# Half-array row scores, value products woven between the scores of a slot, and another buffer in the convolution

## The chip, the cores and the metric

The kernel runs on one core of one Trainium2 chip. The metric is the device time of one execution in microseconds (us), lower is better. Engines: PE (TensorE, matrix products), DVE (VectorE), ACT (ScalarE), POOL (GpSimd), and SP, which issues DMAs.

## What is computed

Two layers over an input of 4 batches x 1024 positions x 256 channels. Layer 0: a long convolution between gates, then a feed-forward network with weights reduced to signs. Layer 1: causal attention with 16 query heads over 4 key heads of 64 channels, then a mixture of experts. Every part stands behind a layer norm and is added to the input through a gate. Cut to the parts that the change touches:

```python
# layer 0, convolution
up = einsum('bld,de->ble', u, in_w) + in_b                  # e = 768: x0, x1, v of 256 channels each
uc = depthwise causal convolution of up with 3 taps, + short_b
vx = v * x1
y = irfft(rfft(vx) * rfft(k)) + vx * filt_bias              # long convolution
out = (y * x0) @ out_w + out_b
# layer 1, attention
scores = einsum('bkgqd,bkpd->bkgqp', qg, k) * scale
probs = softmax(where(causal, scores, -1e30))
out = einsum('bkgqp,bkpd->bkgqd', probs, v)
```

## The kernel before

Batches run one after the other (`for bi in range(B)`), and each engine has its own instruction stream written out by hand; semaphores tie them together. PE's stream in a batch is: convolution, feed-forward, projections, attention, output, experts.

**Attention.** For a head u of 1024 queries the scores are computed twice. `score_rows(u, i)` (L577) computes queries i x 128 to (i + 1) x 128 against the keys up to them, as rows; DVE's `row_maxima` (L1239) takes the row maximum from them. `score_cols(u, c, j)` (L600) computes the transposed scores of keys j x 128 against a half c of 512 queries; the exponential needs the row maximum, which is subtracted by an extra row of the product. Values are split into a high and a low part of fp32r to keep precision: qhh holds the high part of q twice (partitions 0 to 63 and 64 to 127), khl the high part of k over its low part, so that one 128-row product gives q_high x (k_high + k_low); k2 and q2 have 65 rows, k_high over ones and q_low over the negated maxima. Where the block lies on the diagonal, a third product adds the causal mask (L617). The blocks of a head (`BLOCKS`) are 12 slots n = 0 to 11: four key tiles for queries 0 to 511 (512, 384, 256 and 128 columns wide) and eight for queries 512 to 1023 (512 wide five times, 384, 256, 128). Slots 0 to 3 and 8 to 11 carry a mask; slots 3 and 11 are the narrow ones of 128 columns.

`values(u, c, j)` (L620) multiplies the exponentials (high and low part, psplit) with the values (vhi, vlo; 65 columns of weights), in three products (L631, L632, L634) into one of the two banks 0 and 1. It runs four slots behind the scores (`LAG`). `rows_at(u, n)` (L61) says which row scores of later heads a slot takes: tiles 4 to 7 of head u + 1 in slots 0 to 3, tiles 0 to 3 of head u + 2 in slots 8 to 11, one each; in head 0 slots 0 to 3 take two tiles of head 1 each. A row product of over 512 keys is two matmuls into two neighbouring banks. A slot on PE is: scores (high, low, mask), perhaps a projection (L450), row scores, perhaps the transposition of the maxima (L598), three value products of the slot four before. ACT writes each exponential twice (L942, L943); the low part is the difference, on DVE or POOL.

**Convolution.** The six channel tiles of `up` run in the order `E_ORDER`: v of tile 0, x1 of tile 0, v of tile 1, x1 of tile 1, x0 of both. PE projects one (`up_rows`, 12 matmuls), ACT writes it scaled by the last tap (L976), POOL corrects its first two columns (L1534), DVE adds the two other taps in two passes (L1327, L1330). `vx` is v times x1: tile 0 on POOL (L1537), tile 1 on DVE (L1335). There is one buffer x1 for both tiles, so ACT waits at n = 3 for the first product. `gated_rows` on PE (L636) transposes vx for the spectra (L661).

## Time and profile before

| | |
|---|---|
| median of 3 runs | 1879.77 us (1877.68 to 1879.78) |
| profiled execution | 1884.41 us, of which the span from first to last instruction is 1882.6 us |
| mean granted clock of PE in it | 0.968 of full |
| busy: PE, DVE, ACT, POOL | 1764.5, 1431.3, 1000.6, 695.8 us |
| share of PE in the chain that ended last | 65% |

The chain that ended last is followed back from the last instruction to what released each step. PE's recorded duration of a product holds its way through the array too; products overlap in it, so that the distance from start to start is what one costs. "PEld" is the load of weights, which runs beside the product before.

### The profile page before, as it was taken

What the parts mean: (1) busy time and instruction counts of PE and PEld (TensorE: products, weight loads), DVE (VectorE), ACT (ScalarE), POOL (GpSimd) and SP (SyncE); (2) the same over time, 40 slices, a digit from 0 to 9 for tenths busy, and PEclk for the clock granted to TensorE, in tenths of its full rate; (3) what the DMA queues carried; (4) which work ended last, traced back from release to release, by engine and by line L of the source; (5) the groups of instructions that cost most, each with busy time, mean ns of one, the idle gap of its engine ahead of it and who ended that gap; (6) DMA issues with size and microseconds to landing.
All of it is one profiled execution on the core that took longest, in us unless ns stands there. A gap on an engine that the chain in (4) does not pass through costs nothing.

```text
span 1882.6 us, 27319 instructions
## 1 busy us (share of the span) xinstructions
PE 1764.5 (94%) x9228; PEld 1427.0 (76%) x9228; DVE 1431.3 (76%) x2646; ACT 1000.6 (53%) x2162; POOL 695.8 (37%) x725
## 2 busy tenths in 40 slices
PE   8999799999998889999999979999999897999998
PEld 5778577778877767777877867777787785777787
DVE  6788778875678878887468877887656887788754
ACT  2314477676333356777441436777824244777752
POOL 1041444543231344444224144554323324445322
PEclk8999899999999989999999979999999998999999
DMA  7500534432610064343160044444143006354311
GB/s 282 195 7 1 134 108 130 130 69 52 230 56 1 20 168 117 91 133 76 53 250 1 1 118 124 114 102 109 45 169 129 0 1 173 86 135 124 75 30 51
DMA packets 89103, 183.09 MB, mean 97 GB/s; under 512 B 28991, under 2 KB 42111, under 8 KB 85894
## 3 DMA queue, kind: packets, MB, share of 16 engines
q1 hardware_dynamic: 84512, 169.55, 31.1%
q10 hardware_dynamic: 4454, 11.81, 2.0%
q8 instruction: 75, 1.23, 0.3%
q14 instruction: 62, 0.51, 0.1%
HBM read 124.41 MB, written 46.94 MB: 91 GB/s over the span
## 4 chain that ended last, share of the span: by engine, by line
PE 65%; DVE 13%; issue 6%; ACT 5%; DMA 3%; POOL 3%; DVEq 2%; ACTq 2%; SPq 0%; POOLq 0%
PE ps L450 10%; PE ps L591 7%; PE ps L611 7%; PE ps L613 6%; PE ps L634 6%; PE ps L631 6%; PE ps L632 6%; PE ps L804 4%; PE ps L725 3%; PE ps L456 3%; PE ps L680 3%; DVE oT L1260 2%; DVE psplit L1249 2%; PE ps L617 2%; PE ps L548 1%
## 5 line engine op out<-in xcount | busy, mean ns | idle before, releaser
L1239 DVE CUSTOM_DVE_ANT_0 ps<-ps,mrow 128x128 f32<-128x128 f32 (+7 forms) x512 | 385.4, 765 | 104.6 <-PE ps L591 103.0
L1509 POOL TENSOR_TENSOR psplit<-pT,psplit 128x384 fp32r<-128x384 f32 (+3 forms) x320 | 301.9, 957 | 422.6 <-ACT psplit L943 417.5
L943 ACT ACTIVATE psplit<-ps 128x512 fp32r<-128x512 f32 (+3 forms) x768 | 373.0, 486 | 0.0
L942 ACT ACTIVATE pT<-ps 128x512 f32<-128x512 f32 (+3 forms) x512 | 256.2, 500 | 174.0 <-PE ps L617 94.0
L591 PE MATMUL ps<-khl,qhh 128*128 128x512 f32 (+3 forms) x768 | 252.1, 393 | 39.1 <-DMA qhh<-psplit 25.0
L611 PE MATMUL ps<-qhh,khl 128*128 128x512 f32 (+3 forms) x768 | 270.7, 352 | 6.5 <-DMA q<-nmr 6.1
L613 PE MATMUL ps<-q,k 65*128 65x512 f32 (+3 forms) x768 | 268.0, 349 | 0.0
L631 PE MATMUL ps<-psplit,vhi 128*65 128x512 f32 (+3 forms) x768 | 264.2, 344 | 0.0
L634 PE MATMUL ps<-psplit,vhi 128*65 128x512 f32 (+3 forms) x768 | 259.5, 338 | 0.0
L632 PE MATMUL ps<-psplit,vlo 128*65 128x512 f32 (+3 forms) x768 | 259.0, 337 | 0.0
L611 PEld LDWEIGHTS ps<-qhh,khl 128*128 128x128 f32 x768 | 145.3, 189 | 58.3 <-issue 8.7
L591 PEld LDWEIGHTS ps<-khl,qhh 128*128 128x128 f32 x768 | 132.4, 202 | 57.0 <-issue 36.2
L1249 DVE TENSOR_TENSOR psplit<-pT,psplit 128x512 fp32r<-128x512 f32 x192 | 131.1, 707 | 42.3 <-ACT psplit L943 41.4
L942 ACT ACTIVATE mix<-ps 128x512 f32<-128x512 f32 (+2 forms) x256 | 118.1, 461 | 78.2 <-PE ps L613 46.4
L613 PEld LDWEIGHTS ps<-q,k 65*128 65x128 f32 x768 | 145.7, 190 | 17.0
L634 PEld LDWEIGHTS ps<-psplit,vhi 128*65 128x65 f32 x768 | 104.2, 136 | 43.1 <-issue 0.4
L1249 DVE TENSOR_TENSOR psplit<-mix,psplit 128x512 fp32r<-128x512 f32 x128 | 101.5, 793 | 42.1 <-ACT psplit L943 42.1
L632 PEld LDWEIGHTS ps<-psplit,vlo 128*65 128x65 f32 x768 | 104.7, 136 | 34.9
L898 ACT ACTIVATE work<-ps,modb 128x512 f32<-128x512 f32 x48 | 37.3, 778 | 173.5 <-PE ps L548 173.5
L450 PE MATMUL ps<-hT,wqkv 128*128 128x512 f32 x480 | 123.4, 411 | 6.2 <-DVE hT L1150 6.2
L631 PEld LDWEIGHTS ps<-psplit,vhi 128*65 128x65 f32 x768 | 105.5, 137 | 28.5 <-issue 0.3
L1260 DVE TENSOR_TENSOR oT<-work,mix 64x1024 f32<-64x1024 f32 x64 | 94.3, 1474 | 40.5 <-DMA mix<-inverse_scratch 39.6
(211 smaller groups left out, 3302.3 us busy)
## 6 DMA issues: line engine op xcount, KB each, us to landing
qhh<-q_scratch SPq DMA_DIRECT2D x112, 256.0 KB, 5.1
q_scratch<-hrow SPq DMA_DIRECT2D x24, 1024.0 KB, 6.9
mix<-inverse_scratch SPq DMA_DIRECT2D x64, 256.0 KB, 3.5
q<-q_scratch SPq DMA_DIRECT2D x56, 256.0 KB, 4.4
Kf<-kf_scratch SPq DMA_DIRECT2D x3, 3072.0 KB, 17.6
khl<-k_scratch SPq DMA_DIRECT2D x24, 256.0 KB, 7.5
sgn<-sgn_scratch SPq DMA_DIRECT2D x6, 1024.0 KB, 10.7
in_w<-in_w_scratch SPq DMA_DIRECT2D x3, 1536.0 KB, 6.7
```

The lines of the kernel that those rows point to most:

```text
L450: i = mm(o, lhs(a, q), rhs(c, q), start=n == 0, stop=n == len(pairs) - 1)
L591: q = mm(ps[:, b + c // HALF, 0:e - c], qhh[:, r, i * P:(i + 1) * P], khl[:, g % 2, c:e], start=True, stop=True)
L611: mm(ps[:, b, 0:hi - lo], khl[:, g % 2, j * P:(j + 1) * P], qhh[:, r, lo:hi], start=True, stop=False)
L613: i = mm(ps[:, b, 0:hi - lo], k2[:, g % 2, j * P:(j + 1) * P], q2[:, u % 2, lo:hi], start=False, stop=not diagonal)
L631: mm(o, vhi[:, g, j, :], high, start=j == 0, stop=False)
L632: mm(o, vlo[:, g, j, :], high, start=False, stop=False)
L634: mm(o, vhi[:, g, j, :], low, start=False, stop=j == 4 * c + 3).then_inc(s["pv_done"], 1)
L942: A(full(n)[:, 0:hi - lo], ps[:, b, 0:hi - lo], ACT.Exp, scale=SCALE)
L943: A(psplit[:, n % PRING, 0, 0:hi - lo], ps[:, b, 0:hi - lo], ACT.Exp, scale=SCALE)\
L1239: V.tensor_tensor_reduce(out=v, in0=v, in1=mrow[:, L - n:L], scale=1.0, scalar=-3e38, op0=ALU.add, op1=ALU.max, accum_out=mx[:, u % 2, i:i ...
L1249: V.tensor_tensor(psplit[:, n % PRING, 1, 0:m], full(n)[:, 0:m], psplit[:, n % PRING, 0, 0:m].bitcast(F32), ALU.subtract)\
L1509: G.tensor_tensor(psplit[:, n % PRING, 1, 0:m], full(n)[:, 0:m], psplit[:, n % PRING, 0, 0:m].bitcast(F32), ALU.subtract)\
```

## The change

Four things, all in one version. Row scores of heads 1 to 15 use 64 rows of the array, high part by high part only: the low part of the key leaves the row maximum (which only has to be near the maximum, since it cancels in the softmax). Chunks alternate between partitions 0 to 63 (qhh, khl) and 64 to 127 (qhh, k2); k2 and q2 grow to 128 rows for it, with the low products in the upper half, the maximum's row at partition 0 and zeros between. The row tiles 0 to 3 are taken in pairs, in slots 8 and 10. Value products and row scores are woven between the products of a slot (`slot`). In the convolution x1 of tile 1 goes to the buffer work, both vx products are POOL's, and PE's first transposition moves behind the fifth projection.

```diff
...
     else:
-        rows = [(u + 2, n - 8)] if n >= 8 else []
+        rows = [(u + 2, n - 8), (u + 2, n - 7)] if n in (8, 10) else []
     return [(w, i) for w, i in rows if w < HEADS]
...
                 qhh = sb("qhh", [P, QRING, L], F32R, a3)
-                q2 = sb("q2", [HD + 1, 2, L], F32R, a3)
+                q2 = sb("q2", [P, 2, L], F32R, a3)
                 khl = sb("khl", [P, 2, L], F32R, a3)
-                k2 = sb("k2", [HD + 1, 2, L], F32R, a3)
+                k2 = sb("k2", [P, 2, L], F32R, a3)
                 vhi = sb("vhi", [P, KV, NT, HD + 1], F32R, a3)
...
                     .then_inc(q_loaded(1)[0] if h else s["next_loaded"], 16)
-            dma(q2[0:HD, 1, cols].bitcast(F32), one[:, 2:4])\
+            dma(q2[HD:P, 1, cols].bitcast(F32), one[:, 2:4])\
                 .then_inc(q2_loaded(1)[0] if h else s["next_loaded"], 16)
...
-            return {0: x0[:, e % ND, :], 1: x1[:, :], 2: vx[:, e % ND, :]}[e // ND]
+            if e // ND == 1:
+                return x1[:, :] if e % ND == 0 else work[:, 0:2, :].rearrange("p a n -> p (a n)")
+            return (x0 if e // ND == 0 else vx)[:, e % ND, :]
...
                     e = min(n, c + HALF)
-                    q = mm(ps[:, b + c // HALF, 0:e - c], qhh[:, r, i * P:(i + 1) * P], khl[:, g % 2, c:e],
-                           start=True, stop=True)
+                    if u == 0:
+                        rows_of, keys = slice(0, P), khl
+                    elif (c // HALF if n > HALF else i % 2) == 0:
+                        rows_of, keys = slice(0, HD), khl
+                    else:
+                        rows_of, keys = slice(HD, P), k2
+                    q = mm(ps[:, b + c // HALF, 0:e - c], qhh[rows_of, r, i * P:(i + 1) * P],
+                           keys[rows_of, g % 2, c:e], start=True, stop=True)
                 q.then_inc(ready[b], 1)
...
-            def score_cols(u, c, j):
-                g, r = u // GQ, u % QRING
+            def columns(u, c, j):
                 lo, hi = max(c * HALF, j * P), (c + 1) * HALF
...
                     pe.wait_ge(*m_loaded(u))
+                return b, lo, hi
+            def score_high(u, c, j, b, lo, hi):
+                g, r = u // GQ, u % QRING
                 mm(ps[:, b, 0:hi - lo], khl[:, g % 2, j * P:(j + 1) * P], qhh[:, r, lo:hi], start=True, stop=False)
-                diagonal = j * P >= c * HALF
-                i = mm(ps[:, b, 0:hi - lo], k2[:, g % 2, j * P:(j + 1) * P], q2[:, u % 2, lo:hi], start=False, stop=not diagonal)
-                if diagonal:
+            def score_low(u, c, j, b, lo, hi):
+                g, diagonal = u // GQ, j * P >= c * HALF
+                i = mm(ps[:, b, 0:hi - lo], k2[:, g % 2, j * P:(j + 1) * P], q2[:, u % 2, lo:hi], start=False,
+                       stop=not diagonal)
+                if not diagonal:
+                    i.then_inc(ready[b], 1)
+            def score_mask(u, c, j, b, lo, hi):
+                if j * P >= c * HALF:
                     if u == c == j == 0:
                         pe.wait_ge(*at("causal_made", 1))
-                    i = mm(ps[:, b, 0:P], identr[:, :], causal[:, :], start=False, stop=True)
-                i.then_inc(ready[b], 1)
-            def values(u, c, j):
+                    mm(ps[:, b, 0:P], identr[:, :], causal[:, :], start=False, stop=True).then_inc(ready[b], 1)
+            def value(u, c, j, part):
...
                 lo, hi = max(c * HALF, j * P), (c + 1) * HALF
-                if j == 0:
-                    bk.take(pe, ("pv", u, c), until=at("o_done", NHALF * u + c + 1), at=c, counted=False)
-                    if u == c == 0:
-                        pe.wait_ge(*at("v_done", NT // 2))
-                pe.wait_ge(*at("exp_done", n + 1))
+                if part == 0:
+                    if j == 0:
+                        bk.take(pe, ("pv", u, c), until=at("o_done", NHALF * u + c + 1), at=c, counted=False)
+                        if u == c == 0:
+                            pe.wait_ge(*at("v_done", NT // 2))
+                    pe.wait_ge(*at("exp_done", n + 1))
                 o = ps[0:HD + 1, c, lo - c * HALF:HALF]
                 high, low = psplit[:, n % PRING, 0, 0:hi - lo], psplit[:, n % PRING, 1, 0:hi - lo]
-                mm(o, vhi[:, g, j, :], high, start=j == 0, stop=False)
-                mm(o, vlo[:, g, j, :], high, start=False, stop=False)
-                pe.wait_ge(*low_made(n))
-                mm(o, vhi[:, g, j, :], low, start=False, stop=j == 4 * c + 3).then_inc(s["pv_done"], 1)
+                if part == 0:
+                    mm(o, vhi[:, g, j, :], high, start=j == 0, stop=False)
+                elif part == 1:
+                    mm(o, vlo[:, g, j, :], high, start=False, stop=False)
+                else:
+                    pe.wait_ge(*low_made(n))
+                    mm(o, vhi[:, g, j, :], low, start=False, stop=j == 4 * c + 3).then_inc(s["pv_done"], 1)
+            def values(u, c, j):
+                for part in range(3):
+                    value(u, c, j, part)
+            def slot(u, n):
+                cols = BLOCKS[n] + columns(u, *BLOCKS[n])
+                late = NBLK * u + n >= LAG
+                old = (u if n >= LAG else u - 1,) + BLOCKS[n - LAG]
+                narrow = late and cols[4] - cols[3] == P
+                def rows():
+                    for w, i in rows_at(u, n):
+                        score_rows(w, i)
+                score_high(u, *cols)
+                if narrow:
+                    value(*old, 0)
+                    rows()
+                score_low(u, *cols)
+                if narrow:
+                    value(*old, 1)
+                score_mask(u, *cols)
+                if (u, n) in PROJECT_AT:
+                    k = PROJECT_AT[u, n]
+                    project(k, QCOL + (k // 2 - 1) * GQ * HD)
+                if n == TURN_AT and u + 1 < HEADS:
+                    turn_maxima(u + 1)
+                if not narrow:
+                    if late:
+                        value(*old, 0)
+                    rows()
+                    if late:
+                        value(*old, 1)
+                if late:
+                    value(*old, 2)
...
                 for n, e in enumerate(E_ORDER):
-                    if n == 4:
+                    if n == 5:
                         gated_rows(0)
...
                 for u in range(HEADS):
-                    for n, (c, j) in enumerate(BLOCKS):
-                        score_cols(u, c, j)
-                        if (u, n) in PROJECT_AT:
-                            k = PROJECT_AT[u, n]
-                            project(k, QCOL + (k // 2 - 1) * GQ * HD)
-                        for w, i in rows_at(u, n):
-                            score_rows(w, i)
-                        if n == TURN_AT and u + 1 < HEADS:
-                            turn_maxima(u + 1)
-                        if NBLK * u + n >= LAG:
-                            values(u if n >= LAG else u - 1, *BLOCKS[n - LAG])
+                    for n in range(NBLK):
+                        slot(u, n)
                 for n in range(NBLK - LAG, NBLK):
...
                         gated_rows(0)
-                    if n == 3:
-                        act.wait_ge(*at("vx_done", 1))
                     dst = tapped(e)
...
                                            in1=dst[:, 2:L], op0=ALU.mult, op1=ALU.add).then_inc(s["conv_done"], 1)
-                    if n == 3:
-                        dve.drain()
-                        dve.wait_ge(*at("vx_done", 1))
-                        V.tensor_tensor(vx[:, 1, :], vx[:, 1, :], x1[:, :], ALU.mult).then_inc(s["vx_done"], 1)
...
                     G.tensor_tensor(v, v, edge[:, e, :], ALU.add).then_inc(s["edge_done"], 1)
-                    if n == 1:
-                        pool.wait_ge(*at("conv_done", 2))
-                        G.tensor_tensor(vx[:, 0, :], vx[:, 0, :], x1[:, :], ALU.mult).then_inc(s["vx_done"], 1)
+                    if n in (2, 4):
+                        pool.wait_ge(*at("conv_done", n))
+                        dt = n // 4
+                        G.tensor_tensor(vx[:, dt, :], vx[:, dt, :], tapped(ND + dt), ALU.mult).then_inc(s["vx_done"], 1)
                 pool.wait_ge(*at("gates_loaded", 16))
...
                 pool.drain()
-                G.memset(k2[HD:HD + 1, :, :].bitcast(F32), 1.0)
+                G.memset(q2[0:HD, :, :].bitcast(F32), 0.0)
+                G.memset(k2[0:HD, :, :].bitcast(F32), 0.0)
                 pool.drain()
+                G.memset(k2[0:1, :, :].bitcast(F32), 1.0)
+                pool.drain().then_inc(s["pads_made"], 1)
                 pool.wait_ge(*at("h_lo_done", (LN_ATT + 1) * NHALF * ND))
...
                     dma(khl[HD:P, g % 2, cols].bitcast(F32), one[:, 2:4]).then_inc(done, 16)
-                    dma(k2[0:HD, g % 2, cols].bitcast(F32), one[:, 0:2]).then_inc(done, 16)
+                    dma(k2[HD:P, g % 2, cols].bitcast(F32), one[:, 0:2]).then_inc(done, 16)
...
                     one = q_scratch[u // GQ % 2, u % GQ * 32:(u % GQ + 1) * 32]
-                    dma(q2[0:HD, u % 2, :].bitcast(F32), one[:, 2:4]).then_inc(q2_loaded(u)[0], 16)
+                    dma(q2[HD:P, u % 2, :].bitcast(F32), one[:, 2:4]).then_inc(q2_loaded(u)[0], 16)
...
                     sp.wait_ge(*at("nmr_done", u + 1))
-                    dma(q2[HD:HD + 1, u % 2, :].bitcast(F32), nmr[:, u % 2, :].bitcast(F32))\
+                    dma(q2[0:1, u % 2, :].bitcast(F32), nmr[:, u % 2, :].bitcast(F32))\
                         .then_inc(m_loaded(u)[0], 16)
...
                 for h, cols in enumerate(half_of):
-                    dma(k2[0:HD, 0, cols].bitcast(F32), key[h][:, 0:2]).then_inc(s["first_cols"], 16)
-                    dma(q2[0:HD, 0, cols].bitcast(F32), query[h][:, 2:4]).then_inc(s["first_cols"], 16)
+                    dma(k2[HD:P, 0, cols].bitcast(F32), key[h][:, 0:2]).then_inc(s["first_cols"], 16)
+                    dma(q2[HD:P, 0, cols].bitcast(F32), query[h][:, 2:4]).then_inc(s["first_cols"], 16)
                 load_next(dma, 0)
+                sp.wait_ge(*at("pads_made", 1))
                 load_maxima(0)
...
```

## Rows read from the trace of the kernel before

**Rows 1.** The page, part 4: the chain that ended last, shares of the span by engine
```profile
PE 65%; DVE 13%; issue 6%; ACT 5%; DMA 3%; POOL 3%; DVEq 2%; ACTq 2%; SPq 0%; POOLq 0%
```

**Rows 2.** Windows, one head: length, busy PE, PEld, DVE, ACT, POOL; clock, DMA share, GB/s
```profile
380.11:394.15 14.04, 14.04 (x83) 11.20 (x81) 10.80 (x25) 10.76 (x27) 5.57 (x8) 1.00 0.34 77
```

**Rows 3.** Timeline of PE in slot 0 (columns: start, length, engine, line, operands, [idle])
```profile
380.34 0.40 PE L613 MATMUL ps<-q,k 65*128 65x512 f32 x1
...
380.58 0.23 PE L617 MATMUL ps<-causal,identr 128*128 128x128 f32 x1
...
380.64 0.51 PE L591 MATMUL ps<-khl,qhh 128*128 128x512 f32 x2
...
380.99 0.39 PE L631 MATMUL ps<-psplit,vhi 128*65 128x512 f32 x1
```

**Rows 4.** Timeline of PE and its weight loads in the narrow slot 3
```profile
384.13 0.22 PE L611 MATMUL ps<-qhh,khl 128*128 128x128 f32 x1
384.14 0.19 PEld L613 LDWEIGHTS ps<-q,k 65*128 65x128 f32 x1
384.19 0.28 PE L613 MATMUL ps<-q,k 65*128 65x128 f32 x1
384.25 0.19 PEld L617 LDWEIGHTS ps<-causal,identr 128*128 128x128 f32 x1
...
384.31 0.27 PE L617 MATMUL ps<-causal,identr 128*128 128x128 f32 x1
...
384.42 0.69 PE L591 MATMUL ps<-khl,qhh 128*128 128x512 f32 x2
...
384.94 0.22 PE L631 MATMUL ps<-psplit,vhi 128*65 128x128 f32 x1
...
385.06 0.22 PE L634 MATMUL ps<-psplit,vhi 128*65 128x128 f32 x1
...
385.20 0.50 PE L611 MATMUL ps<-qhh,khl 128*128 128x512 f32 x1
```

**Rows 5.** Timeline of the set-up where 64-row and 128-row products meet, PE and loads
```profile
16.87 1.91 PE L497 MATMUL ps<-sine,fw 64*64 64x512 f32 x2
...
18.71 0.29 PEld L472 LDWEIGHTS ps<-cT,spare 128*128 128x128 f32 x1 [1.61 <-issue]
...
35.97 0.30 PEld L472 LDWEIGHTS ps<-cT,Kf 128*128 128x128 f32 x2
36.29 0.18 PEld L532 LDWEIGHTS ps<-fwo,sine 64*128 64x128 f32 x1
...
41.36 1.06 PE L532 MATMUL ps<-fwo,sine 64*128 64x256 f32 x2
...
42.35 0.09 PEld L482 LDWEIGHTS ps<-Kf,cT 128*4 128x4 f32 x2 [0.65 <-issue]
```

**Rows 6.** Timeline of the convolution of the second batch
```profile
530.40 2.38 POOL L1537 TENSOR_TENSOR vx<-vx,x 128x1024 f32<-128x1024 f32 x1 [3.90 <-DVE x L1330]
...
532.82 1.45 ACT L976 ACTIVATE x<-ps,tap_b,short_w 128x512 f32<-128x512 f32 x2 [2.50 <-POOL vx L1537]
...
535.76 7.35 PE L450 MATMUL ps<-hT,in_w 128*128 128x512 f32 x24 [1.83 <-DVE vx L1330]
...
538.35 1.23 DVE L1335 TENSOR_TENSOR vx<-vx,x 128x1024 f32<-128x1024 f32 x1
...
544.56 7.14 PE L661 MATMUL ps<-vrow,fwd 128*128 128x256 f32 x32 [0.57 <-ACT vrow L962]
```

**Rows 7.** Timeline of POOL before attention: the one-row fill and the next work
```profile
636.99 1.80 POOL L1563 MEMSET k<- 1x2048 f32 x1
642.96 1.30 POOL L1516 TENSOR_TENSOR oT<-oT 128x512 f32<-128x512 f32 x1 [4.17 <-DVE hT L1150]
```

**Rows 8.** Timeline where a one-column fp32r product follows a 128-column one
```profile
484.90 0.59 PE L804 MATMUL ps<-wo,oT 128*128 128x256 f32 x2
...
485.12 0.35 PEld L450 LDWEIGHTS ps<-wr,first 128*1 128x1 f32 x4
```

More of the change, by code:

```diff
@@ L87 @@
         "w1_split": 2, "x_done": 1, "tap_made": 1, "edge_done": 6, "gates_mixed": 1, "bias_added": 6, "y_pool": 3,
-        "causal_made": 1, "rope_done": 9, "v_done": 4, "low_pool": 112, "x_loaded": 16,
+        "causal_made": 1, "pads_made": 1, "rope_done": 9, "v_done": 4, "low_pool": 112, "x_loaded": 16,
         "gates_loaded": 16, "first_rows0": 64, "first_cols": 64, "first_rows1": 64, "m_loaded0": 128,
@@ L325, in adaln_hyena_binffn_gqa_moe @@
                  "m_loaded1", "v_copied",
-                 "exp_done", "causal_made", "low_pool", "low_dve", "pv_done", "o_done", "sum_loaded", "inverse_done",
+                 "exp_done", "causal_made", "pads_made", "low_pool", "low_dve", "pv_done", "o_done", "sum_loaded", "inverse_done",
                  "inverse_stored", "inverse_loaded", "oT_done", "top_done", "w1_loaded0", "w1_loaded1",
```

## The prediction

> **What bounds the kernel now.** The profiled execution took 1884.41 us (span 1882.6); the median of the runs shown is 1879.77, 0.25% less. I sum changes in microseconds and add them to either. A difference under about 0.2% (4 us) can't be told from none here.
>
> I read the chain that ended last first: TensorE (PE) holds 65% of it, VectorE (DVE) 13% [rows 1]. Then the stretches: one attention head in its steady state, without a projection, is 14.04 us long, PE is busy for all 14.04 us at the full clock, while DVE has 10.80 and ScalarE (ACT) 10.76 us of work [rows 2]. There are 64 heads (16 in each of 4 batches), so attention is about half of the kernel, it is bound by PE alone, and what a head loses or gains on PE is the kernel's, up to some 3 us a head before another engine decides.
>
> Next, what a matmul costs PE there. Start to start is the price, not the recorded duration: a 512-column product starts 0.24 us before the next one [rows 3] though it is recorded with 0.39 to 0.40; the part beyond it is the way through the array. I take 0.23 for 512 columns, 0.175 for 384, 0.12 for 256 (interpolated) and 0.06 for 128 (384.13 to 384.19) [rows 4]. The same rows show a second price. The mask product starts 0.12 after a 128-column one, the rows product 0.11 after the mask, the next slot 0.14 after the last 128-column value product: weights of 128 columns are loaded 0.11 us apart (384.14, 384.25), and such a load begins when the previous product starts. So a 128-column product followed by 128 columns of weights costs 0.11 instead of 0.06; followed by 65 columns of weights (value products) it costs 0.06 (384.94 and 385.06 are two such steps apart). One head before has 30 + 6 products of 512 columns, 12 of 384, 12 of 256 and 21 of 128: 8.28 + 2.10 + 1.44 + 1.26 = 13.08 us. The 0.96 us left of 14.04 are 14 such load stalls (3 in slot 3: high to low, low to mask, value to next high; 2 in slot 11; 1 after slot 7; 8 from mask to row scores). By the rows a stall is 0.05 us, by this balance at most 0.068; I take 0.057.
>
> **Weaving (orders of products inside a slot).** After the change a wide slot runs high, low, mask, value 0, rows, value 1, value 2, and a narrow one high, value 0, rows, low, value 1, mask, value 2. The mask is now followed by 65 columns of weights, a narrow high by value 0. In a batch the mask stood before row scores 15 x 4 + 14 x 4 = 116 times, all gone; a narrow high stood before low 32 times, gone; low before mask is gone in slot 11 (16), in slot 3 value 1 before mask keeps it. That is 164 stalls. In slot 3 value 0 (128 columns) now stands before the row scores, 15 new ones, unless another cost swallows them (next part). 164 x 0.057 = 9.3 us a batch, **-37 us** in all; by the two bounds of a stall -33 to -45.
>
> **Half-array row scores.** For heads 1 to 15 each 128-row product becomes a 64-row one, alternately on partitions 0 to 63 and 64 to 127, each into its own bank. Two terms are not shown by any 64-row row of attention, since it has none.
> (a) Overlap of the two halves. Bounds: none (the products follow each other at 0.23 as now), or full (the shorter one is free). With full overlap and no other cost a head saves 0.06 (tiles 0, 1) + 0.175 (2, 3) + 0.06 + 0.12 + 0.175 + 0.23 (tiles 4 to 7) = 0.82 us; 15 x 4 x 0.82 = -49 us. I take full overlap, since nothing shared between the halves is in the rows, and keep 0 for the range.
> (b) The change between whole and half array. The nearest rows are the set-up's 64-row products [rows 5]. The last of them that precedes 128-row work ends at 18.78 (16.87 + 1.91), and the next weights are loaded only at 18.71, 0.07 before that end, with no semaphore on it; again 42.35 against the end 42.42. Everywhere in attention the next load starts at the start of the product before it (384.13, 384.14) [rows 4]. The other way, the last 128-row load before 36.29 starts at 36.08, so its product streams at 36.19, and the first 64-row load waits to 36.29. In all three the array runs empty before the next weights go in: 0.10 us of gap at full clock (a 0.40 us record, less 0.07, less the 0.23 stream), and then the load itself (0.06 or 0.11 us), which was hidden before, lies open.
> The Trainium skill (TensorEngine Tiling (Array Packing), Key Properties) says that tiles operate independently but that changing the tiling mode drains TensorE; by its first half alone the change gains, by both it comes out as in this sum, and the trace agrees with the second half by those 0.07 us.
>
> With it a group of row scores costs 0.10 + max(0.11 + Ta, 0.22 + Tb) (two loads one after the other, then two streams beside each other), and on leaving 0.10 + 0.06 before value 1, or 0.10 + 0.11 before low in slot 3. Tiles 4, 5, 6, 7: 0.44 + 0.44 + 0.495 + 0.55 on entering and streaming, 3 x 0.16 + 0.21 on leaving, 2.615 us against 0.29 + 0.35 + 0.405 + 0.46 = 1.505 before: +1.11. Tiles 0 and 1: 0.60 against 0.18, +0.42. Tiles 2 and 3: 0.71 against 0.405, +0.305. A head: +1.835 us. Head 1 has its eight tiles in four groups: +0.42, +0.305, +0.19, +0.07, about +1.0. A batch: 14 x 1.835 + 1.0 = 26.7 us, **+107 us** in all. Without overlap (tiles 4 to 7: +0.425, tiles 2, 3: +0.07 a head) 30 us more. These groups swallow the 15 new stalls.
>
> **Convolution.** Before, ACT waited 2.50 us at 532.82 for GpSimd's (POOL) 2.38 us product at 530.40, because the second x1 overwrites the first; PE then waited 1.83 us at 535.76, DVE did the second product (1.23 us at 538.35) between two passes, and PE reached the spectra at 544.56 [rows 6]. Now x1 of tile 1 goes to work and both products are POOL's. DVE passes I put at 1.3 us each, a little over its 1.23 us product of the same length, two for a channel tile. Tile 2 starts at 530.4, when the pass that releases POOL's product ends, and no longer behind that product (532.8), and ends at 533.0; PE's fifth projection can start there (2.8 us for 12 products) and transposes 0 follow; tile 3 needs its edge behind POOL's product (532.8), ends at 535.7; PE's sixth runs 537.0 to 539.8; POOL's second product runs 535.7 to 538.1, transposes 1 end at 540.9, ACT copies two banks, and the spectra start at about 541.7. That is 2.8 us earlier, and DVE's next work waits on it: 4 x 2.8 = **-11 us**, bounded by 0 (POOL's product slowed beside DVE) and -14.
>
> **Edits at nothing.** POOL now fills two 64 x 2048 regions more; the one-row fill of the same length takes 1.80 us, and POOL then idles 4.17 us before its next work [rows 7], which covers 2 x 1.8 = 3.6; without that cover up to 3.6 us a batch would come late to the first rotation. SP's wait for that signal stands ahead of the first load of the maxima, which needs the first head's row scores and they need POOL's rotations after the fills, so it waits for nothing. DMAs keep their number and sizes. Pairing row tiles at slots 8 and 10 changes nothing for DVE, which has 3.2 us free in a head [rows 2].
>
> **Sum:** 107 - 37 - 11 = +59 us. Profiled execution 1943.4, median 1938.8 us: slower.
>
> **Rivals.**
> R1, free change and full overlap: -49 for the halves; weaving then keeps the 15 new stalls, 149 x 0.057 x 4 = -34; convolution -11: -94, 1786 us. For it: both loads of a pair fit under the 0.23 us of value 0; also at 485.12 the weights of a one-column product are loaded right at the start of the product before it (484.90 + 0.59 - 0.38 = 485.11) [rows 8], so some changes of a product's form cost nothing. Against it: that is a change in columns, at fp32r; the changes in rows all show the gap [rows 5]. Their products are fp32, though, and attention's fp32r, which is why this rival keeps weight. The point at which it decides: 14 x 12 + 8 = 176 changes a batch, 704 in all, against 94 us: under 0.134 us a change the kernel is faster, over it slower; the rows give 0.16 to 0.21.
> R2, no overlap and free change: 64 rows merely cost what 128 do; -34 - 11 = -45, 1835 us.
> R3, gap without overlap: +59 + 30, 1968 us.
> R4, a smaller gap (about 0.13 us a change): near nothing, 1880 us.
> The Trainium skill (TensorE: Matmul & The Clock Gate, Part 3) gives 3.07 times the speed for four 32-row tiles, a steady run inside one mode; no run here shows overlap, and if it were half as good the sum would lie between the forecast and R3.
>
> **Chances:** forecast 0.50, R1 0.20, R2 0.15, R3 0.08, R4 0.07. The forecast's own range is 1920 to 1955 (stall bounds, convolution 0 to -14, gap 0.08 to 0.12). Leaving out R1, the range is 1820 to 1975. Faster: 0.20 + 0.15 + 0.02 = 0.37; same 0.05; slower 0.50 + 0.08 = 0.58.
>
> **What will show it.** Half-array loads that start at the recorded end of the value product less 0.07 us, and value 1's load likewise after the rows: gap right. Two row products with starts 0.11 apart and durations that overlap fully: overlap right; 0.23 apart: R2 or R3. Mask to value 0 in 0.06 us: weaving right. A steady head of 14.04 + 1.84 - 0.63 = 15.2 us (R1 12.6, R2 13.4). Spectra 2.8 us nearer to the first projection. PE idle in attention behind DVE or ACT would show that another engine decides, and my sum would be wrong in kind.

## The result, and the profile after

The changed kernel takes 1895.55 us (median of 4 runs, 1894.01 to 1898.71) against 1879.24 us before in the same comparison: ratio 1.009, 95% interval 1.0073 to 1.0108, so 16.3 us slower. The profiled execution took 1894.01 us. The sign was forecast, the size was not: +59 was predicted.

The page of the changed kernel: busy time by engine (part 1), the chain that ended last (part 4), the two groups of row products (part 5: busy, mean ns of one, idle before).

```profile
PE 1777.8 (94%) x9228; PEld 1362.0 (72%) x9228; DVE 1427.2 (75%) x2642; ACT 1004.7 (53%) x2162; POOL 722.1 (38%) x737
...
PE 67%; DVE 14%; issue 6%; ACT 3%; DVEq 3%; DMA 3%; ACTq 2%; POOL 2%; POOLq 0%; SPq 0%
...
L599 PE MATMUL ps<-khl,qhh 64*128 64x512 f32 (+6 forms) x408 | 182.4, 468 | 36.8 <-DMA qhh<-psplit 26.1
...
L599 PE MATMUL ps<-k,qhh 64*128 64x256 f32 x360 | 151.0, 419 | 0.0
```

The bound is the same as in [rows 1]: PE. L599 is the row score, L623, L628 and L638 are high, low and mask, L653, L655 and L658 values 0, 1 and 2. One steady head, to be held against [rows 2]:

```profile
374.24:388.84 14.60, 14.60 (x82) 10.28 (x81) 10.80 (x24) 10.74 (x29) 5.73 (x7) 1.00 0.40 112
```

PE is recorded busy throughout at the full clock, DVE and ACT have the same work as before. A second way to measure a head, used below for every version, is the row of the transpositions of the maxima, one a head: with five of them, first start to last start is four heads. Before and after (count, ns min/median/max, first and last start):

```profile
L598 PE MATMUL ps<-identr,nm x5: 272/273/273, 387.9 to 444.1; 128*8 128x128 f32 x5
```

```profile
L606 PE MATMUL ps<-identr,nm x5: 271/271/273, 388.8 to 447.4; 128*8 128x128 f32 x5
```

56.2 / 4 = 14.05 us a head before, 58.6 / 4 = 14.65 after: +0.60, where +1.2 was forecast.

Summed over the four batches, from first to last of these transpositions (15 intervals each), attention takes 942.8 us after and 923.5 before. Interval by interval (mean of four batches, after less before) the plain heads lose 0.44 to 0.62. The fifth and ninth interval, which hold a projection and took 17.5 us before, lose 0.68 and 0.70. The two right behind those gain 0.17 and 0.15. The first and fourth gain 0.5 and 0.8; in them PE waits 0.5 to 2.2 us at a time for DMA, DVE or ACT, and the difference scatters between batches of one execution, from -1.6 to +1.9 us in the first and from -2.2 to 0 in the fourth.

**The array empties at each change, and the halves overlap.** Slots 2 and 3 of the changed kernel, PE:

```profile
384.17 0.28 PE L653 MATMUL ps<-psplit,vhi 128*65 128x256 f32 x1
384.38 0.50 PE L599 MATMUL ps<-khl,qhh 64*128 64x512 f32 x1
384.38 0.44 PE L599 MATMUL ps<-k,qhh 64*128 64x384 f32 x1
384.80 0.33 PE L655 MATMUL ps<-psplit,vlo 128*65 128x256 f32 x1
...
385.15 0.22 PE L653 MATMUL ps<-psplit,vhi 128*65 128x128 f32 x1
385.30 0.49 PE L599 MATMUL ps<-khl,qhh 64*128 64x512 f32 x1
385.31 0.50 PE L599 MATMUL ps<-k,qhh 64*128 64x512 f32 x1
385.74 0.33 PE L628 MATMUL ps<-q,k 128*128 128x128 f32 x1
```

The weight loads beside them:

```profile
384.38 0.18 PEld L599 LDWEIGHTS ps<-khl,qhh 64*128 64x128 f32 x1
384.38 0.18 PEld L599 LDWEIGHTS ps<-k,qhh 64*128 64x128 f32 x1
384.80 0.13 PEld L655 LDWEIGHTS ps<-psplit,vlo 128*65 128x65 f32 x1 [0.24 <-issue]
```

Value 0 starts at 384.17 and streams 0.12, to 384.29; its record ends at 384.45. The half-array loads start at 384.38: 0.07 before the recorded end, as in [rows 5], and 0.09 after the stream. On leaving, the load at 384.80 stands 0.08 before the recorded end of the longer row product (384.88), so the second emptying is there too. Both row products start at 384.38 and run together; and so do both loads, which the prediction had put one after the other. The group costs from 384.29 until value 1 streams (384.80 + 0.055): 0.565 us (0.57 with the starts to the nanosecond). The next one, before low, costs 385.74 + 0.105 - 385.21 = 0.635.

**The convolution** of the second batch, after (against [rows 6]):

```profile
524.22 11.20 PE L452 MATMUL ps<-hT,in_w 128*128 128x512 f32 x48
...
533.60 2.39 POOL L1586 TENSOR_TENSOR vx<-vx,x 128x1024 f32<-128x1024 f32 x1 [1.18 <-DVE x L1382]
533.60 1.28 DVE L1379 SCALAR_TENSOR_TENSOR vx<-ps,short_w,vx 128x1023 f32<-128x1023 f32 x1
...
536.30 3.06 PE L452 MATMUL ps<-hT,in_w 128*128 128x512 f32 x12 [0.89 <-DVE vx L1382]
...
539.04 2.39 POOL L1586 TENSOR_TENSOR vx<-vx,work 128x1024 f32<-128x1024 f32 x1
...
539.99 2.98 PE L452 MATMUL ps<-hT,in_w 128*128 128x512 f32 x12
...
544.42 7.14 PE L724 MATMUL ps<-vrow,fwd 128*128 128x256 f32 x32 [0.57 <-ACT vrow L1016]
```

ACT's wait of 2.50 us for POOL is gone, PE waits 0.89 instead of 1.83, and DVE goes on at 533.60 beside POOL's product. From PE's first projection to the spectra: 20.20 us; before it was 544.56 - 521.02 = 23.54, with the first projection at

```profile
521.02 11.20 PE L450 MATMUL ps<-hT,in_w 128*128 128x512 f32 x48
```

Part of the difference is TensorE's clock. The last two projections took 7.35 us before (535.76 to 543.11) and take 3.06 + 2.98 = 6.04 now. The windows of the two stretches (length, busy PE, PEld, DVE, ACT, POOL; clock, DMA share, GB/s), before and after:

```profile
535.76:543.11 7.35, 7.35 (x26) 5.91 (x27) 5.41 (x5) 3.20 (x5) 0.40 (x3) 0.77 0.00 0
```

```profile
536.30:544.42 8.12, 7.55 (x41) 6.22 (x41) 5.67 (x5) 4.73 (x8) 4.48 (x6) 1.00 0.05 20
```

Behind PE's wait of 1.83 us the mean granted clock was 0.77 before, a mix of the two levels of 1.2 and 2.4 GHz; behind the wait of 0.89 us it is 1.00. That is 1.3 of the 3.34 us.

### The profile page after: what moved, and what is told of

Read it like the earlier page. It is cut to its first block, busy times and chain, and to the rows that moved or that the text cites. A ratio compares the mean times of both kernels' runs of the same rounds, so it can differ in the third digit from the quotient of the medians.

```text
span 1892.2 us, 27327 instructions
## 1 busy us (share of the span) xinstructions
PE 1777.8 (94%) x9228; PEld 1362.0 (72%) x9228; DVE 1427.2 (75%) x2642; ACT 1004.7 (53%) x2162; POOL 722.1 (38%) x737
## 4 chain that ended last, share of the span: by engine, by line
PE 67%; DVE 14%; issue 6%; ACT 3%; DVEq 3%; DMA 3%; ACTq 2%; POOL 2%; POOLq 0%; SPq 0%
PE ps L452 10%; PE ps L655 9%; PE ps L623 7%; PE ps L628 7%; PE ps L658 6%; PE ps L653 6%; PE ps L599 6%; PE ps L858 4%; PE ps L788 3%; PE ps L743 3%; DVE psplit L1301 2%; DVE gT L1419 2%; PE ps L638 2%; DVE ps L1291 2%; DVE oT L1312 1%
## 5 line engine op out<-in xcount | busy, mean ns | idle before, releaser
L1557 POOL TENSOR_TENSOR psplit<-pT,psplit 128x384 fp32r<-128x384 f32 (+3 forms) x320 | 309.3, 976 | 434.6 <-ACT psplit L997 433.5
L1291 DVE CUSTOM_DVE_ANT_0 ps<-ps,mrow 128x128 f32<-128x128 f32 (+7 forms) x512 | 379.2, 775 | 120.6 <-PE ps L599 119.1
L623 PE MATMUL ps<-qhh,khl 128*128 128x512 f32 (+3 forms) x768 | 271.3, 353 | 8.6 <-DMA q<-nmr 4.4
L655 PE MATMUL ps<-psplit,vlo 128*65 128x512 f32 (+3 forms) x768 | 273.0, 355 | 0.0
L628 PE MATMUL ps<-q,k 128*128 128x512 f32 (+3 forms) x768 | 265.9, 346 | 0.0
L653 PE MATMUL ps<-psplit,vhi 128*65 128x512 f32 (+3 forms) x768 | 263.1, 343 | 0.0
L658 PE MATMUL ps<-psplit,vhi 128*65 128x512 f32 (+3 forms) x768 | 259.1, 337 | 0.1
L599 PE MATMUL ps<-khl,qhh 64*128 64x512 f32 (+6 forms) x408 | 182.4, 468 | 36.8 <-DMA qhh<-psplit 26.1
L623 PEld LDWEIGHTS ps<-qhh,khl 128*128 128x128 f32 x768 | 144.3, 188 | 53.1 <-DVE mx L1291 11.1
L628 PEld LDWEIGHTS ps<-q,k 128*128 128x128 f32 x768 | 144.8, 189 | 27.3 <-issue 13.7
L655 PEld LDWEIGHTS ps<-psplit,vlo 128*65 128x65 f32 x768 | 103.7, 135 | 83.7 <-issue 53.8
L599 PEld LDWEIGHTS ps<-khl,qhh 64*128 64x128 f32 (+1 forms) x408 | 78.4, 199 | 107.3 <-issue 77.6
L599 PE MATMUL ps<-k,qhh 64*128 64x256 f32 x360 | 151.0, 419 | 0.0
L1301 DVE TENSOR_TENSOR psplit<-mix,psplit 128x512 fp32r<-128x512 f32 x128 | 106.7, 833 | 42.0 <-ACT psplit L997 42.0
L653 PEld LDWEIGHTS ps<-psplit,vhi 128*65 128x65 f32 x768 | 104.2, 136 | 25.2
## 6 DMA issues: line engine op xcount, KB each, us to landing
Kf<-kf_scratch SPq DMA_DIRECT2D x3, 3072.0 KB, 17.5
```

What stands on the lines that cost most here:

```text
L599: q = mm(ps[:, b + c // HALF, 0:e - c], qhh[rows_of, r, i * P:(i + 1) * P], keys[rows_of, g % 2, c:e], start=True, stop=True)
L623: mm(ps[:, b, 0:hi - lo], khl[:, g % 2, j * P:(j + 1) * P], qhh[:, r, lo:hi], start=True, stop=False)
L628: i = mm(ps[:, b, 0:hi - lo], k2[:, g % 2, j * P:(j + 1) * P], q2[:, u % 2, lo:hi], start=False, stop=not diagonal)
L653: mm(o, vhi[:, g, j, :], high, start=j == 0, stop=False)
L655: mm(o, vlo[:, g, j, :], high, start=False, stop=False)
L658: mm(o, vhi[:, g, j, :], low, start=False, stop=j == 4 * c + 3).then_inc(s["pv_done"], 1)
```

## The experiments

**e1_conv.** The kernel before with the convolution's part alone: x1 of tile 1 in work, both products on POOL, the first transposition behind the fifth projection.

```diff
-            return {0: x0[:, e % ND, :], 1: x1[:, :], 2: vx[:, e % ND, :]}[e // ND]
+            if e // ND == 1:
+                return x1[:, :] if e % ND == 0 else work[:, 0:2, :].rearrange("p a n -> p (a n)")
+            return (x0 if e // ND == 0 else vx)[:, e % ND, :]
...
```

> Only the convolution's part of the change, on the kernel before. In the changed kernel the spectra start 3.35 us earlier after the first projection in each batch, but 3.8 us in all come back later, before attention. Theory A (the give-back belongs to the convolution's own new order, so that what follows the spectra waits for something else): -9.6 us, 1869.6. Theory B (it belongs to the fills and the new layout of attention's buffers): -13.4 us, 1866. Attention heads stay at 14.04 us in both.

Measured: 1864.49 us, ratio 0.9918 (0.9892 to 0.9943), which is -15.4 us (the two medians, 1882.07 and 1864.49, lie 17.6 apart). Attention kept its head:

```profile
L600 PE MATMUL ps<-identr,nm x5: 272/273/273, 386.1 to 442.3; 128*8 128x128 f32 x5
```

14.05 us. The stretch from projection to spectra fell from 94.0 to 80.8 us over the four batches, -13.1, so the whole shift arrives at the end; nothing is given back. The other 2 to 4 us are inside the interval. The convolution's part is thus a gain, and the rest of the change costs 1.009 - 0.9918 = 1.7%, 32 us.

**e2_full.** The changed kernel with all row scores on 128 rows: weaving, pairing and convolution without half arrays.

```diff
-                    if u == 0:
+                    if True:
                         rows_of, keys = slice(0, P), khl
```

> The changed kernel with all row scores on the whole array, 128 rows against khl: the weaving, the pairs, the fills and the convolution stay, no product of attention uses 64 rows. Theory A (each change between whole and half array costs what the groups show, the weaving gains its load stalls): a head of 14.04 - 11 x 0.06 = about 13.35 us, 60 x 0.69 = 41 us less in attention and about 10 in the convolution: 1829 us. Rival B (another engine decides once PE is that fast): PE idles behind DVE or ACT, head at 13.7 or more, 1850 us or more.

Measured: 1859.73 us, ratio 0.988 (0.9849 to 0.9911).

```profile
L606 PE MATMUL ps<-identr,nm x5: 271/272/273, 384.9 to 439.8; 128*8 128x128 f32 x5
```

13.73 us a head, 0.32 less than without weaving, where 11 stalls of 0.057 should have given 0.63. By count only 9 of the 14 stalls are gone here: in slot 3 value 0 stands ahead of the row scores, and inside the pair the 128 columns of tile 0 stand ahead of tile 1's weights. 9 x 0.052 = 0.47. The end of slot 3 takes part of it back. DVE there, PE's next load, and PE:

```profile
395.66 0.14 DVE L1291 DVE_READ_ACCUMULATOR2_ANT mx<- 128x1 f32 x1
```

```profile
395.85 0.19 PEld L623 LDWEIGHTS ps<-qhh,khl 128*128 128x128 f32 x1
```

```profile
395.63 0.22 PE L658 MATMUL ps<-psplit,vhi 128*65 128x128 f32 x1
395.86 0.50 PE L623 MATMUL ps<-qhh,khl 128*128 128x512 f32 x1
```

From value 2 to the next high 0.23 us instead of 0.14 [rows 4]: PE waits for a bank until DVE has read the row maximum out (395.66 + 0.14), and loads 0.05 later. The kernel before already had this wait, and so has the changed one, there a shorter one:

```profile
385.00 0.14 DVE L1239 DVE_READ_ACCUMULATOR2_ANT mx<- 128x1 f32 x1
385.19 0.19 PEld L611 LDWEIGHTS ps<-qhh,khl 128*128 128x128 f32 x1
```

```profile
385.94 0.14 DVE L1291 DVE_READ_ACCUMULATOR2_ANT mx<- 128x1 f32 x1
386.13 0.19 PEld L623 LDWEIGHTS ps<-qhh,khl 128*128 128x128 f32 x1
```

Its size is read from the start of value 2 in slot 3 to the start of the low product of slot 4, as a mean over 32 heads (eight of each batch): 0.345 us in e3_noweave, e4_upper and e7_groups, which do not wait there, 0.48 in the kernel before, 0.40 in the changed kernel, 0.56 here. So the wait is 0.14, 0.05 and 0.22 us a head. Here it grew by 0.08, which leaves 0.39 of the 0.47; the last 0.07 stay open.

The two heads of a batch with a projection that took 17.5 us take 18.2, as in the changed kernel. So at the kernel's level weaving with pairs gave only 1859.73 against 1864.49, and the intervals of the two ratios overlap.

**e3_noweave.** The changed kernel with the slot in its old order: high, low, mask, projection, rows, transposition, values; the half arrays and pairs stay.

```diff
-                if narrow:
-                    value(*old, 0)
-                    rows()
...
-                if narrow:
-                    value(*old, 1)
...
+                rows()
...
-                if not narrow:
-                    if late:
-                        value(*old, 0)
-                    rows()
-                    if late:
-                        value(*old, 1)
                 if late:
-                    value(*old, 2)
+                    values(*old)
```

> The changed kernel with the order of products inside a slot as before (high, low, mask, row scores, values), the half-array row scores, pairs and convolution stay. Theory A (a group of half-array rows costs the same wherever it stands, and swallows the load stall behind the mask): a head of 14.04 + 1.29 - 0.45 - 0.05 = 14.85 us, some 1910 to 1920 us. Rival B (the place between value products is what keeps a group cheap): head at 15.3 us, 1940 us.

Measured: 1899.81 us, ratio 1.0098 (1.007 to 1.0126).

```profile
L606 PE MATMUL ps<-identr,nm x5: 271/272/272, 391.6 to 450.4; 128*8 128x128 f32 x5
```

14.70 us: beside half-array groups weaving is worth 0.05 us a head. An array that runs empty before it loads hides the stall between mask and row scores (a mask at 386.86 and its group at 387.02, which is the mask's 0.06 and the emptying), and the pairing had already taken the other two of those eight places. What is left for weaving is 3 stalls, 0.16 us. Against them stand the load of 128 instead of 65 columns behind the group of slot 3 (0.05) and the wait for the bank at the end of slot 3, which this version does not have (0.05).

**e4_upper.** The changed kernel with every 64-row product on partitions 0 to 63: same products, same changes, no overlap possible.

```diff
-                    elif (c // HALF if n > HALF else i % 2) == 0:
+                    elif True:
```

> The changed kernel with every half-array product on partitions 0 to 63, so that no two lie in different halves; number and place of the changes between whole and half array stay. Theory A (two halves overlap fully, loads and streams): the shorter product of each pair is paid, 0.06 + 0.12 + 0.175 + 0.23 + 0.11 + 0.175 = +0.87 us a head, 15.5 us, 1946 us. Rival B (no real overlap, the records only look so and the gap was smaller than thought): as the changed kernel, 14.6 us a head and 1895 us.

Measured: 1936.2 us, ratio 1.0289 (1.0251 to 1.0327).

```profile
L606 PE MATMUL ps<-identr,nm x5: 271/272/273, 396.9 to 458.7; 128*8 128x128 f32 x5
```

15.45 us a head. Slot 2 of one, PE:

```profile
407.28 0.28 PE L653 MATMUL ps<-psplit,vhi 128*65 128x256 f32 x1
407.49 0.67 PE L599 MATMUL ps<-khl,qhh 64*128 64x512 f32 x2
408.09 0.34 PE L655 MATMUL ps<-psplit,vlo 128*65 128x256 f32 x1
```

The same group as at 384.17 takes 0.60 from load to load instead of 0.42: the 0.175 us of the shorter product lie open again. So the overlap is real, it is worth 0.80 us a head and 37 (by the ratios) to 41 us (by the medians) of the kernel, and without it the change would have been slower by 2.9%.

**e5_single.** e2_full with `rows_at` of before: row tiles 0 to 3 one by one in slots 8 to 11.

```diff
-        rows = [(u + 2, n - 8), (u + 2, n - 7)] if n in (8, 10) else []
+        rows = [(u + 2, n - 8)] if n >= 8 else []
```

> As the version with all row scores on the whole array, but tiles 0 to 3 again one by one in slots 8 to 11. In that version PE waited at the end of slot 3 for a bank that a row maximum on DVE holds (some 0.11 us a steady head, up to 0.75 in heads with a projection). Theory A (that wait comes from slots 0 to 3, where row scores are now issued one value product later): only the load stall inside the pair goes, head 13.69 - 0.05 = 13.64 us, the heads with a projection stay at 18.2. Rival B (DVE is late because of the pairs): those heads return to 17.2, some 10 us less in all.

Measured: 1855.82 us, ratio 0.9855 (0.9831 to 0.9879).

```profile
L606 PE MATMUL ps<-identr,nm x5: 271/271/273, 387.8 to 442.5; 128*8 128x128 f32 x5
```

13.68 us, and the heads with a projection are back at 17.5 to 17.6. The waits of PE's weight loads in one such interval, from transposition to transposition (total, times, longest), first with pairs (e2_full, 338.13 to 356.30):

```profile
PEld ps L623 <- DVE mx L1291: 1.8, 3, 1.0
```

Then with singles (341.73 to 359.32):

```profile
PEld ps L623 <- DVE mx L1291: 0.7, 1, 0.7
PEld ps L599 <- DVE mx L1291: 0.5, 1, 0.5
```

With the pairs PE waits 0.6 us longer for the banks that DVE's row maxima hold. That is worth 0.6 us in each of the eight heads of this kind, 5 us, though the 95% intervals of the two versions overlap; the steady head barely cares. That it is bunching as such is not shown: e7_groups below has four tiles at once in slot 8, and its heads with a projection take 17.5 us.

**e6_half_small.** Row tiles 4 to 7 on 128 rows, only tiles 0 to 3 on half arrays.

```diff
-                    if u == 0:
+                    if u == 0 or i >= 4:
```

> The changed kernel with half-array row scores for tiles 0 to 3 alone (slots 8 and 10, four changes between whole and half array a head), tiles 4 to 7 on the whole array. Theory A (a pair costs by itself what it costs in the changed kernel, 0.457 and 0.57 us against 0.177 + 0.05 and 0.405 on the whole array): head 13.69 + 0.23 + 0.165 = 14.08 us, 60 x 0.39 = 24 us over the version without any half array. Rival B (small pairs pay, the large tiles are the loss): head at 13.69 or less.

Measured: 1872.67 us, ratio 0.994 (0.9923 to 0.9957).

```profile
L606 PE MATMUL ps<-identr,nm x5: 271/272/273, 389.3 to 445.8; 128*8 128x128 f32 x5
```

14.13 us: two groups cost 0.40 over e2_full. By the trace of after they cost 0.46 and 0.57, against 0.18 and 0.405 of plain products: 0.44. The price per group adds up as read.

**e7_groups.** Fewer changes of form: the eight row tiles in three half-array groups a head instead of six.

```diff
-        rows = [(u + 1, AHEAD + n)]
+        rows = [(u + 1, AHEAD + n - 1), (u + 1, AHEAD + n)] if n in (1, 3) else []
     else:
-        rows = [(u + 2, n - 8), (u + 2, n - 7)] if n in (8, 10) else []
+        rows = [(u + 2, i) for i in range(4)] if n == 8 else []
```

> The changed kernel with its half-array row scores in three groups a head instead of six: tiles 4 and 5 in slot 1, 6 and 7 in slot 3, 0 to 3 in slot 8. Theory A (each group pays 0.09 + 0.10 on entering and 0.09 + 0.05 on leaving, and nothing else): 14.61 - 3 x 0.33 = 13.6 us a head, some 60 us less than the changed kernel. Rival B (DVE cannot take two large tiles in a row before their banks are wanted): PE waits for banks, head at 14.0 us or more.

Measured: 1882.44 us, ratio 1.0012 (0.9998 to 1.0027).

```profile
L606 PE MATMUL ps<-identr,nm x5: 271/272/273, 390.7 to 446.4; 128*8 128x128 f32 x5
```

13.93 us, 0.7 less than in the changed kernel. Slot 3 on PE, and the waits of its loads from 390 to 450 us (total, times, longest):

```profile
400.56 0.50 PE L599 MATMUL ps<-khl,qhh 64*128 64x512 f32 x1
400.56 0.44 PE L599 MATMUL ps<-k,qhh 64*128 64x384 f32 x1
401.12 0.47 PE L599 MATMUL ps<-khl,qhh 64*128 64x512 f32 x1
401.13 0.50 PE L599 MATMUL ps<-k,qhh 64*128 64x512 f32 x1
```

```profile
PEld ps L599 <- DVE mx L1291: 1.4, 4, 0.4
```

The second tile of the group starts 0.56 after the first, where a stream takes 0.23: it waits for a bank that DVE's row maximum holds, 1.4 us in these four heads. Without those 0.35 the head would be 13.58, as the price per group has it. A third of what fewer changes give goes to the banks.

The kernel is only 13 us faster than the changed one, where 60 had been expected, and 23 us slower than e2_full. 18 us of it are in one interval a batch, the fourth, which takes 22.7 us instead of 18.2. There the group in slot 8 belongs to the first head of the next key head:

```profile
263.42 0.44 PE L599 MATMUL ps<-khl,qhh 64*128 64x128 f32 x1 [3.77 <-issue]
```

It waits 3.0 to 4.7 us in the four batches (0.5 to 0.8 in the changed kernel), and after it the granted clock is down, with a mean of 0.50, 0.59, 0.73 and 0.73 over the next 6.3 us. The window behind the first of these waits (columns as in [rows 2]):

```profile
263.42:269.70 6.28, 6.28 (x21) 4.46 (x22) 2.56 (x10) 1.53 (x4) 1.74 (x2) 0.50 0.08 26
```

At 0.50, which is 1.2 GHz, these 6.28 us of products cost twice what they cost elsewhere. What the group waits for the profile does not name; by the code it is a bank or the loads of the new head's queries and keys, of which the queries' were issued at 258.08 here and at 256.54 in the changed kernel.

**e8_late** and **e9_but3.** e2_full with single row tiles, and the old order in the slots where PE was seen to wait: slots 0 to 3, or slot 3 alone.

```diff
+                if n < 4:
+                    score_high(u, *cols)
+                    score_low(u, *cols)
+                    score_mask(u, *cols)
+                    rows()
+                    if late:
+                        values(*old)
+                    return
```

For e9_but3 the condition is `n == 3`.

> A version for use: convolution changed, row scores on the whole array and one by one, order inside slots 0 to 3 as before, woven only in slots 4 to 11. Theory A (six load stalls of 0.052 us go, and DVE gets its row scores in slots 0 to 3 as early as before): head 14.04 - 0.31 = 13.73 us, heads with a projection at 17.2, some 18 us less than the convolution alone: ratio to before 0.982. Rival B (DVE sets the pace of the projection heads anyway): as the version woven throughout, ratio 0.988.

> As the version woven only in slots 4 to 11, but slots 0 to 2 woven too; only slot 3 keeps the old order. It tells whether DVE's lateness comes from row scores issued one value product later in slots 0 to 2, or from slot 3. Theory A (slot 3 alone: there two products of 512 columns and DVE's longest row maximum stand before the next slot's bank): three stalls less, head 13.73 - 0.16 = 13.57 us, ratio to before 0.980. Rival B (every slot's delay adds up on DVE): PE waits for a bank at the end of slot 3 again, head at 13.65 to 13.75, ratio 0.985.

Measured: 1855.33 us, ratio 0.9852 (0.9835 to 0.9868), and 1855.27 us, ratio 0.9856 (0.9832 to 0.988). The heads, e8_late and then e9_but3:

```profile
L606 PE MATMUL ps<-identr,nm x5: 272/272/273, 383.5 to 438.4; 128*8 128x128 f32 x5
```

```profile
L606 PE MATMUL ps<-identr,nm x5: 272/272/273, 385.2 to 439.9; 128*8 128x128 f32 x5
```

13.73 and 13.68 us, and neither beats e5_single by anything that can be measured: what the order of slots 0 to 3 saves, PE meets again as a wait for the row maxima. At the end of slot 3 that wait is 0.14 us in e8_late, 0.25 in e9_but3 and 0.22 in e5_single, measured as under e2_full. Slot 3 has the old order in the first two of them, so it is the row scores issued later in slots 0 to 2 that bring the longer wait, as rival B of e9_but3 has it. The 17.2 us expected for e8_late's projection heads were 17.5. These three have the lowest medians of all versions run (e2_full's interval overlaps theirs), 1.5% under the kernel before: the convolution's part gives about 0.8, weaving without pairs and without half arrays the other 0.6 to 0.7.

## Why the prediction was right or wrong

**That PE alone sets a head.** Right, with a limit that was there from the start. A steady head is PE's own work but for the end of slot 3, where PE waits 0.14 us before and 0.05 after for the bank of a row maximum. The prediction took that place (385.06 to 385.20) for a load stall; its balance of 14 equal stalls in 0.96 us held this wait too, which is part of why it came out at 0.068 where a stall is 0.052. And "up to some 3 us a head before another engine decides" was wrong: in three of the four versions whose head is 0.3 to 0.4 us below 14.05 that wait grows to 0.22 to 0.25 (e2_full, e5_single, e9_but3; in e8_late it stays at 0.14). DVE's total was not the limit, its place in the head was.

**The gap at a change of form.** Right: it is there on entering and on leaving, 0.09 us each (0.10 predicted), with the new weights' load open behind it (0.055 for 65 columns, 0.105 for 128). It was read off set-up products in fp32; the row scores are fp32r and behave the same, so the reservation under R1 has fallen. R1 and R2, the two cases without it, are out. The Trainium skill (TensorEngine Tiling (Array Packing), Key Properties) says that a change of mode drains TensorE; 384.38 against 384.29 is that drain here.

**Overlap.** Right, shown by e4_upper (0.80 us a head; 0.82 was predicted). R3 is out for this kernel; its case, built in e4_upper, takes 1936 us, not the 1968 forecast.

**The cost of a group: the step that failed.** The formula was 0.10 + max(0.11 + Ta, 0.22 + Tb) + 0.10 + 0.06, with "two loads one after the other". Both loads start together, so it is 0.09 + 0.11 + max(Ta, Tb) + 0.09 + 0.055. Read from the trace, tiles 4 to 7 cost 0.58, 0.565, 0.57 and 0.63 (predicted 0.60, 0.60, 0.655 and 0.76), the pairs 0.457 and 0.57 (0.60 and 0.71): 3.37 a head instead of 3.925, against 2.09 before. The loss is 1.28 us a head, not 1.835; over 14 heads of four batches the difference is 31 us, most of the error of 43. Having taken the products as independent I had no row to take the loads as dependent: [rows 4] shows loads 0.11 apart that go to the same rows of the array. The Trainium skill (TensorEngine Tiling (Array Packing), Key Properties), the section from which the prediction has the independent tiles, says that different tiles can load weights and multiply in parallel; the two loads at 384.38 agree. The Trainium skill (TensorE: Matmul & The Clock Gate, Part 3) says that a load of weights overlaps running products only when its row group differs. [rows 4] do not bear that out: the load at 384.14 starts 0.01 us after a product that runs on all 128 rows.

**Weaving.** The count of 164 stalls a batch was right for the changed kernel (11 in a steady head), and the 15 new ones were swallowed. A stall reads 0.052, not 0.057. Attributing the gain to weaving was wrong: e3_noweave shows that beside half-array groups 8 of the 11 go away by the emptying and the pairing. The sum 14.05 + 1.28 - 11 x 0.052 = 14.76 is 0.11 above the measured 14.65. Of that, 0.08 is the wait for the bank at the end of slot 3, 0.14 us before and 0.05 after; 0.03 stay open.

**From a head to the kernel.** The loss was multiplied by all heads. The two heads behind a projection waited for something else before (14.8 us instead of 14.05) and lose nothing, and the first and fourth wait for other engines and DMA: 4 of 15 intervals pay nothing. With the corrected price the sum would be 14 x 4 x 1.28 + some 3 for head 1 - 34 = +41 for attention. Between first and last transposition the two traces show 25 for after against e1_conv, 16 less: four such intervals a batch leave out some 10 (16 x 0.6; together they differ by -0.8), and the shorter wait at slot 3 some 4 (44 x 0.08). Another 6 us lie between spectra and first transposition, a stretch that takes 480 to 486 us in any version, so they may be scatter; with them the sum of the two, 31 us, is nearly the 32 by the ratios. Taken together: 59 - 31 (price of a group) - 10 (intervals that pay nothing) - 4 (slot 3) - 2 (convolution) + 6 = 18 us, where 16.3 were measured.

**Convolution.** Predicted -11, measured -13.1 in the stretch and -15.4 by the ratio, 20.20 us for 23.54 instead of 2.8 less. POOL's product isn't slowed beside DVE (2.39 against 2.38), DVE's pass takes 1.28 (1.3 assumed). What was mis-sized is the end. PE's sixth projection ends at 542.97 and the spectra start at 544.42, 1.45 us later, as before (543.11 to 544.56); the prediction had 1.9 (539.8 to 541.7). POOL's second product ends at 541.43, ahead of the sixth projection's end. The prediction did not name the clock behind the old wait: its 2.8 us for 12 products is a full-clock figure, and so the 1.3 us were in its sum without being seen.

**Edits at nothing.** The fills cost nothing that shows:

```profile
636.45 1.80 POOL L1612 MEMSET q<- 64x2048 f32 x1
638.20 1.94 POOL L1613 MEMSET k<- 64x2048 f32 x1
```

The two take 3.7 us, under the 4.17 us of [rows 7]; from spectra to first transposition e2_full, which has them, takes 480.8 us over four batches and e1_conv, which hasn't, 479.7. "Pairing changes nothing for DVE" was wrong: e2_full against e5_single puts 0.6 us on each of the 17.5 us heads with a projection.

**Rival R4** (a smaller gap, about 0.13 us a change) came nearest to the time, but not for its reason: the gap was as large as forecast, and the load behind it was paid once for two.

## What to carry to other kernels

A change between whole-array and half-array products costs about 0.09 us plus an open load of weights, each way, and two halves of 512 columns save only 0.23: group many half-array products between two changes, or leave the form alone. Six groups a head lost 0.92 us against whole-array products and three lost 0.2; every version with half arrays ran slower than e2_full, which has none. An engine that a page shows 100% busy can still wait, as PE did here for 0.14 us a head: look where a start comes later than its neighbours of the same shape. Before multiplying a saving by the heads, look at which heads wait for something else, and at whose bank the engine meets when it comes earlier: the place of another engine's work in the loop counts, not its total. When four edits come as one, run them apart: here one was worth -0.8%, one -0.6%, one cost more than both (2.1%), and one was within the noise.

## What the runs showed of the hardware beyond that

Loads of weights for two different row halves of the array run at the same time: both recorded at 384.38 and at 385.30, 0.18 us each, while loads to the same rows stand 0.11 apart [rows 4]. Two 64-row products of 512 columns on different halves start within 0.01 us of each other and last 0.49 and 0.50; on the same half (e4_upper) the pair takes 0.67 instead of 0.50 for its record. Nothing in these runs shows one half slowing the other.
